# Scores of the second attention through M = Wq^T Wk, low halves of turn 1 on GpSimd, routing weights stationary

## The reference, cut to what matters

```python
x = x + _L0_xattn_ref(ctx_1024, _layernorm(x), ...)      # 8 heads of 128, keys of context and x
x = x + _L0_ffn_ref(_layernorm(x), W1, b1, W2, b2, scale)  # 256 -> 1024 -> 256, gelu, rank-one updates
x = x + _L1_xattn_ref(_layernorm(x), ctx_1024, ctx_1024, Wq_w, Wq_b, Wk_w, Wk_b, Wv_w, Wv_b)
x = x + _L1_ffn_ref(_layernorm(x), Wg, Wu, Wd, Wr, temperature)
...
Q = jnp.einsum('bsd,kd->bsk', query, Wq_w) + Wq_b        # _L1_xattn_ref: one head of 256
K = jnp.einsum('bsd,kd->bsk', key_, Wk_w) + Wk_b
V = jnp.einsum('bsd,vd->bsv', value, Wv_w) + Wv_b
attn = jax.nn.softmax(jnp.einsum('bqk,bsk->bqs', Q, K) * scale, axis=-1)
...
weights = _routing_weights(x, Wr, temperature)           # _L1_ffn_ref: x @ Wr is 256 x 8 per image
h = jax.nn.silu(x @ Wg[e]) * (x @ Wu[e])                 # 8 experts of 256, all of them, in every row
out = jnp.einsum('bte,betd->btd', weights, e_out)
```

## Time and profile before

| what | value |
|---|---|
| time, median of 3 runs (lowest to highest) | 2014.67 us (2013.67 to 2015.39) |
| the profiled execution's own time | 2019.56 us |
| its span in the trace | 2017.8 us |
| TensorE busy | 1953.7 us, 97% of the span, 14272 matmuls |
| VectorE, ScalarE, GpSimd busy | 1386.3, 1105.1, 362.4 us |
| granted clock of TensorE, mean | 0.99 |

### The profile page before, as it was taken

The page is one execution under the profiler, slowest core; times in us unless marked ns, Lnnn a source line. Parts: engine busy times, 40 slices in busy tenths (PEclk is TensorE's granted clock), DMA queues, the critical chain, the costliest instruction groups (busy, mean ns, idle before and its releaser), DMA issues.

```text
span 2017.8 us, 41686 instructions
## 1 busy us (share of the span) xinstructions
PE 1953.7 (97%) x14272; PEld 1832.0 (91%) x14272; DVE 1386.3 (69%) x3420; ACT 1105.1 (55%) x2283; POOL 362.4 (18%) x613
## 2 busy tenths in 40 slices
PE   7999999999999999999978799999999999999998
PEld 6789888888888888888878799999999999999998
DVE  7876767767777777677646656766666667666665
ACT  5655556555555556555555445544554555544553
POOL 2222222222222222222211101111111001111100
PEclk9999999999999999999989899999999999999999
DMA  4000000000000000000014000000000000000000
GB/s 160 12 22 21 10 10 21 21 21 10 10 21 21 21 10 10 21 21 10 6 38 137 11 13 17 11 17 15 13 16 16 17 11 17 11 17 11 16 7 11
DMA packets 47211, 44.51 MB, mean 22 GB/s; under 512 B 6848, under 2 KB 45376, under 8 KB 47168
## 3 DMA queue, kind: packets, MB, share of 16 engines
q1 hardware_dynamic: 47168, 43.96, 6.9%
HBM read 34.77 MB, written 8.39 MB: 21 GB/s over the span
## 4 chain that ended last, share of the span: by engine, by line
PE 86%; DVE 5%; ACT 5%; issue 2%; SPq 1%; POOL 0%; DMA 0%; ACTq 0%; DVEq 0%; POOLq 0%
PE ring L618 9%; PE ring L620 9%; PE ring L619 9%; PE ring L1749 8%; PE ring L1750 8%; PE ring L1751 8%; PE ring L671 4%; PE sim L1749 3%; PE sim L1751 3%; PE sim L1750 3%; PE sim L618 3%; PE sim L620 2%; PE sim L619 2%; PE ps_x L1749 2%; PE ps_x L1750 2%
## 5 line engine op out<-in xcount | busy, mean ns | idle before, releaser
L1749 PE MATMUL ring<-b_xch,b_weh 128*128 128x256 f32 x1024 | 294.0, 287 | 18.9 <-DVE b_wel L1376 15.8
L1750 PE MATMUL ring<-b_xcl,b_weh 128*128 128x256 f32 x1024 | 289.4, 283 | 0.0
L1751 PE MATMUL ring<-b_xch,b_wel 128*128 128x256 f32 x1024 | 289.3, 283 | 0.0
L411 ACT ACTIVATE a_pr<-sim,a_nmax 128x512 f32<-128x512 f32 x256 | 174.4, 689 | 209.4 <-DVE a_nmax L537 209.3
L326 POOL TENSOR_SCALAR a_pr<-a_pr,a_rinv 128x512 f32<-128x512 f32 x256 | 183.0, 728 | 500.3 <-DVE a_rinv L547 497.5
L1749 PEld LDWEIGHTS ring<-b_xch,b_weh 128*128 128x128 f32 x1024 | 196.9, 192 | 20.3 <-DVE b_wel L1376 16.9
L1750 PEld LDWEIGHTS ring<-b_xcl,b_weh 128*128 128x128 f32 x1024 | 197.1, 193 | 0.0
L1751 PEld LDWEIGHTS ring<-b_xch,b_wel 128*128 128x128 f32 x1024 | 196.4, 192 | 0.0
L1387 DVE TENSOR_TENSOR b_act_e<-b_act_e,ring 128x512 f32<-128x512 f32 x128 | 88.0, 688 | 134.5 <-PE ring L1751 121.1
L1117 ACT ACTIVATE b_act_e<-ring 128x512 f32<-128x512 f32 x128 | 76.6, 599 | 169.1 <-PE ring L1751 168.7
L528 DVE TENSOR_TENSOR a_ptl<-ring,a_pth 128x512 fp32r<-128x512 f32 x256 | 163.6, 680 | 3.1 <-ACT a_pth L401 2.0
(11 more groups left out here) (355 smaller groups left out, 6285.9 us busy)
## 6 DMA issues: line engine op xcount, KB each, us to landing
a_c_in<-in_ctx_in SPq DMA_DIRECT2D x16, 256.0 KB, 2.7
a_x_in<-in_x SPq DMA_DIRECT2D x16, 256.0 KB, 2.9
a_x_res<-in_x SPq DMA_DIRECT2D x16, 256.0 KB, 2.7
x_between<-a_x_out SPq DMA_DIRECT2D x16, 256.0 KB, 2.2
b_x_s<-x_between SPq DMA_DIRECT2D x16, 256.0 KB, 2.6
b_up<-b_ev SPq DMA_DIRECT2D x256, 1.0 KB
out_x<-b_acc SPq DMA_DIRECT2D x16, 256.0 KB, 2.2
b_ct_raw<-in_ctxT SPq DMA_DIRECT2D x15, 256.0 KB, 2.6
```

Of the source, the lines that this page charges most:

```text
L411: nc.scalar.activation(pr[:, h % 2, t, :], sim[t][:], ACT.Exp, bias=nmax[:, h % 2, t:t + 1], accum_out=rsum[:, h % 2, t:t + 1]).then_inc(e ...
L1749: nc.tensor.matmul(out, lh, rh, start=(n == 0), stop=False)
L1750: nc.tensor.matmul(out, lh, rl, start=False, stop=False)
L1751: last = nc.tensor.matmul(out, ll, rh, start=False, stop=(n == len(parts) - 1 and not more))
```

## The change

- **M.** With Q = x Wq^T + bq and K = c Wk^T + bk the scores are (x M + u) c^T, u = Wk^T bq, plus a number for each row of the query, x v + s. M = Wq^T Wk, u, v and s are formed once (`fold`, 18 matmuls for v and the sums and 12 for M, where image 0's keys were), and M takes Wq's place in the queries' product (`q_fill`). The keys' product and its halves are gone; the scores' moving operand is cth, ctl. The row number cancels in the softmax; the kernel forms it on GpSimd (`row_shifts`) and ScalarE (`row_shift_sums`) and VectorE adds it to the maximum and takes it off again (`maxima`).
- **Turn 1.** `expert_low` of experts 2 to 7 moves from VectorE to GpSimd's queue, experts 2 to 5 ahead of rstd B, 6 ahead of rstd A, 7 ahead of the odd rows. Their high halves move one slot ahead (`WARM_AT`), the first ahead of silu 1.
- **Routing.** Wr, its halves in 16 of 128 columns and zeros behind, is the stationary operand: 4 matmuls with 256 columns ahead of expert 0's gate, a copy by ScalarE (`r_copy`) and 2 transposes (`r_turned`) behind its up.
- **Order.** `v_fill` moves from behind `y_update` to behind gate 4, and its halves to the slot of silu 4. In the passage image 0's fourth gelu moves from ahead of head 2's probabilities to behind K4, and the context's split from head 2 to head 4.

```diff
...
-    Q, K, V, PT = (slice(n, n + 3, 2) for n in (0, 1, 4, 5))
...
+    Q, V, PT = (slice(n, n + 3, 2) for n in (1, 4, 5))
+    mh, (wk_raw, ml) = put("w_queries", "mh", [P, DC, D], F32R, odd=1), put("w_queries", "ml", [P, DC, D], F32R, raw=True,
+                                                                        odd=1)
...
+    cth, (wq_raw, ctl) = put("w_queries", "cth", [P, DC, S], F32R, odd=0), put(
+        "w_queries", "ctl", [P, DC, S], F32R, raw=True, odd=0)
+    once = {"K": (wk_raw, mh, ml), "Q": (wq_raw, cth, ctl), "V": (wv_raw, wvh, wvl)}
+    v_b, rt = put("w_queries", "v_b", [P, D]), put("w_queries", "rt", [P, S])
+    wr = put("w_queries", "wr", [P, DC, P], F32R)
+    bk_wide = xth[:].rearrange("p c (z m) -> p c z m", z=2)
...
-    WARM_AT = {2: 0, 3: 1, 4: 2, 5: 3, 6: 4, 7: 5}
+    WARM_AT = {2: 0, 3: 1, 4: 2, 5: 2, 6: 3, 7: 4}
...
+        def row_shifts(n):
+
+            pool.wait_ge(ln_ready["B"], n + 1)
+            nc.gpsimd.tensor_tensor(pr[:], ln[:], v_b[:].unsqueeze(1).to_broadcast([P, ST, D]), ALU.mult)\
+                .then_inc(shift_in, 1)
...
+            if (h, done) == (3, "probs"):
+                pool.wait_ge(first.sems["ring_full"], first.fill_count(2, ("Q", 3)))
+                nc.gpsimd.memset(f32(wr[:]), 0.0).then_inc(consts, 1)
+                pool.wait_ge(w_ready, 6)
+                pool.wait_ge(consts, 3)
+                nc.gpsimd.tensor_copy(wr[:, :, 0:2 * E].rearrange("p c (z e) -> p c z e", z=2), f32(wr_two[:]))\
+                    .then_inc(consts, 1)
+                pool.wait_ge(full["H", 3], 1)
+                nc.gpsimd.tensor_copy(bk_wide, f32(bqk[:, 1]).unsqueeze(3).to_broadcast([P, DC, 2, P]))\
+                    .then_inc(consts, 1)
             if (h, done) == (4, "probs"):
+                pool.wait_ge(uv_step, 2)
+                row_shifts(0)
                 bias_x2(0)
...
             def turn(t, chain, more, warm):
+                if warm:
+                    for e in (2, 3, 4, 5):
+                        expert_low(e)
                 if chain:
                     rstd_of(t, "B")
+                    row_shifts(t)
                     bias_x2(t)
+                if warm:
+                    expert_low(6)
                 if more:
                     rstd_of(t + 1, "A")
                     bias_x1(t + 1)
+                if warm:
+                    expert_low(7)
+                if more:
                     odd_rows(t + 1)
...
+        def folded_high():
+            act.wait_ge(m_full, 2)
+            nc.scalar.activation(mh[:], halves(OWN["M"]), ACT.Copy, scale=QSCALE).then_inc(wqkv_hi, 1)
+
+        def row_shift_sums(t):
+            act.wait_ge(shift_in, t + 1)
+            for k in range(ST):
+                last = nc.scalar.activation(pr[:, k, :], pr[:, k, :], ACT.Identity, bias=shift[:, 0:1],
+                                            accum_out=row_shift[:, k:k + 1])
+            last.then_inc(shift_ready, 1)
...
+
+        def r_copy(t):
+            act.wait_ge(full["R"], 2 * t + 1)
+            nc.scalar.activation(rt[:], ring[BANK["R"]][:, 0:S], ACT.Copy).then_inc(hi["R"], 1)
...
-            if (h, done) == (2, "begin"):
+            if (h, done) == (2, ("K", 4)):
                 gelu_high(0, 3)
-            if (h, done) == (2, ("T", 2, 1)):
-                context_high(0)
...
             if (h, done) == (4, ("K", 6)):
-                biased_high(0, "K", K, bk_s)
+                folded_high()
+                context_high(0)
...
             if (h, done) == (5, "exps"):
-                biased_high(0, "Q", Q, bq_s)
+                act.wait_ge(uv_step, 2)
+                row_shift_sums(0)
+                queries_high(0)
...
+                r_copy(0)
...
+                for e in warm_in(0) if warm else ():
+                    for j in range(3):
+                        expert_high(e, j)
                 silu(i, 1)
                 routing_exps(i)
                 hidden_high(i, 1)
                 if chain:
-                    for n in range(HC // 2):
-                        gelu_high(t, n)
-                for e in warm_in(0) if warm else ():
-                    for j in range(3):
-                        expert_high(e, j)
-
-                silu(i, 2)
-                if chain:
-                    context_high(t)
-                hidden_high(i, 2)
+                    gelu_high(t, 0)
+                    gelu_high(t, 1)
                 for e in warm_in(1) if warm else ():
                     for j in range(3):
                         expert_high(e, j)
                 if chain:
+                    gelu_high(t, 2)
+                    gelu_high(t, 3)
...
+                for e in warm_in(2) if warm else ():
+                    for j in range(3):
+                        expert_high(e, j)
...
-                if chain:
-                    biased_high(t, "K", K, bk_s)
-                    copy_high(t, "V", hh[:, V, 0:S])
...
                 for e in warm_in(3) if warm else ():
                     for j in range(3):
                         expert_high(e, j)
...
+                if chain:
+                    copy_high(t, "B", xth[:])
+                    copy_high(t, "V", hh[:, V, 0:S])
+                hidden_high(i, 4)
+                for e in warm_in(4) if warm else ():
+                    for j in range(3):
+                        expert_high(e, j)
+                if chain:
+                    queries_high(t)
+                    row_shift_sums(t)
...
+        def folded_biases():
+
+            dve.wait_ge(m_full, 1)
+            nc.vector.tensor_scalar(v_b[:], OWN["UV"][:, 0:D], QSCALE, None, ALU.mult)
+            nc.vector.tensor_reduce(sums[:], OWN["UV"][:, D:D + 6].rearrange("p (n z) -> p n z", z=2), AX.X, ALU.add)\
+                .then_inc(uv_step, 1)
+            dve.wait_ge(uv_step, 1)
+            nc.vector.tensor_scalar(shift[:], sums[:, 0:1], QSCALE / D, None, ALU.mult)
+            nc.vector.tensor_scalar(sums[:, 1:3], sums[:, 1:3], QSCALE, None, ALU.mult).then_inc(uv_step, 1)
+
+        def folded_low():
+            dve.wait_ge(wqkv_hi, 4)
+            nc.vector.scalar_tensor_tensor(ml[:], halves(OWN["M"]), QSCALE, f32(mh[:]), ALU.mult, ALU.subtract)\
+                .then_inc(wqkv_lo, 1)
...
+            dve.wait_ge(max_ready, 2 * t + 1)
+            dve.wait_ge(shift_ready, t + 1)
+            for k in range(ST):
+                last = nc.vector.scalar_tensor_tensor(peak[:, k:k + 1], nmax[:, k:k + 1], row_shift[:, k:k + 1],
+                                                      row_shift[:, k:k + 1], ALU.subtract, ALU.add)
+            last.then_inc(max_ready, 1)
...
             if (h, done) == (4, ("K", 6)):
                 norm_apply(0, "B", x2_s)
-                biased_low(0, "K", K, bk_s)
+                folded_biases()
+                folded_low()
+                context_low(0)
...
             if (h, done) == (4, ("T", 4, 1)):
+                dve.wait_ge(shift_in, 1)
                 norm_apply(1, "A", x1_s)
...
-                for e in warm_in(0) if warm else ():
-                    for j in range(3):
-                        expert_low(e, j)
...
                 if chain:
-                    biased_low(t, "K", K, bk_s)
                     norm_apply(t, "B", x2_s)
-                    copy_low(t, "V", hl[:, V, 0:S], hh[:, V, 0:S])
...
                 if chain:
                     copy_low(t, "B", xtl[:], xth[:])
+                    copy_low(t, "V", hl[:, V, 0:S], hh[:, V, 0:S])
                 hidden(i, 4)
                 if more:
+                    dve.wait_ge(shift_in, t + 1)
                     norm_apply(t + 1, "A", x1_s)
                 hidden_low(i, 4)
-                for e in warm_in(3) if warm else ():
...
                 if chain:
-                    biased_low(t, "Q", Q, bq_s)
+                    queries_low(t)
...
+        def fold():
+
+            v, sums_at = OWN["UV"][:, 0:D], OWN["UV"][:, D:D + 6]
+            product(v, range(DC), lambda c: bk_wide[:, c, 0, :], lambda c: bk_wide[:, c, 1, :], lambda c: cth[:, c, :],
+                    lambda c: ctl[:, c, :])
+            for n in range(3):
+                for c in range(DC):
+                    for z, w in enumerate((mh, ml)):
+                        st = bk_wide[:, c, z, :] if n == 0 else w[:, c, (n - 1) * P:n * P]
+                        last = nc.tensor.matmul(sums_at[:, 2 * n:2 * n + 2], st, bqk[:, 0, c, :],
+                                                start=(c == 0 and z == 0), stop=(c == DC - 1 and z == 1))
+            last.then_inc(m_full, 1)
+            cd = halves(OWN["M"])
             for k in range(DC):
                 cols = slice(k * P, (k + 1) * P)
-                last = product(cd[:, k, :], range(DC), lambda c: wqkvh[:, w, c, cols], lambda c: wqkvl[:, w, c, cols],
-                               lambda c: rh[:, c, :], lambda c: rl[:, c, :])
-            last.then_inc(full[name], 1)
```

(43 more changed lines are left out.)

162 lines of the change are left out of this document (69 added, 93 removed).

## The result

The changed kernel takes 1989.37 us (median of 4 runs, 1987.67 to 1991.09); the kernel before, timed beside it, 2015.03 (2013.67 to 2017.28). The ratio is 0.987, 95% interval 0.986 to 0.9884: 25.7 us less, where 30 were forecast (1984.7, range 1966 to 2003). The profiled executions stand 28.5 us apart in their spans (2017.8 and 1989.3), since the one of before lay 4.5 us above its median and the one of after 1.7.

A forecast was written before the change was run, and what follows sets the result against it. TensorE, busy 97% of a 2017.8 us span, was taken as the bound; gains of 13.0 (loop turns 2 to 15), 16 (turn 1) and 1 (passage) make 30 us off the 2014.67 median: 1984.7 us, range 1966 to 2003.

The forecast's parts named there:

- The bound: Whole kernel: TensorE, busy 97% of 2017.8 us, sets the time; busy time removed counts in full wherever it doesn't wait.
- Loop: routing 0.13 us: Loop turns 2 to 15: the new routing product with 2 transposes saves TensorE 0.13 us per turn.
- Loop: a new wait at transposes B of 0.60 us: Loop turns: TensorE arrives earlier at transposes B and waits 0.60 us for VectorE's normalisations, leaving 0.93 us gain per turn.
- Costs put at nothing: Loop: row shifts on GpSimd, row sums on ScalarE and the maximum correction lie in idle time and cost nothing.
- Turn 1: 68 us: Second loop's turn 1: falls from 84.3 to 68 us, a gain of 16, with two long waits of 2.5 and 4.5.
- The clock term: Turn 1: each us of long wait costs 0.75 us more through the lower clock; 7.0 us of waits cost 5.2.
- 24 (no long wait): Turn 1: the upper end of its forecast gain, 24 us, if no long wait comes.
- Passage: a gain of 1: Passage between the halves: M's longer chain against the moved fourth gelu, net gain 1 us, ends 4 lost and 4 gained.
- (2): Loop and turn 1: neither the wait at B nor the one at the scores comes; gain 46, 1968 us, chance 0.20.
- (3): GpSimd's SBUF lock stalls VectorE: turn 1 gives 8 and the loop 5 us; 2001 us, chance 0.20.
- (4): Loop: keys' matmuls were hidden, a VectorE and ScalarE chain sets the turn; only turn 1 gains; 1998 us, chance 0.05.
- (5): Turn 1: GpSimd's rounding subtraction costs far more than its addition; slower overall from 3.8 us each; chance 0.05.

## Why the prediction was right, point by point

- **The bound.** Right. TensorE's matmuls count in full (twelve put back: +1.41 less the wait they fill). My window for a turn ended 0.26 us short of the next routing product (56.66 instead of 56.92 us); in the differences this cancels, but "55.7 us per turn" should have read 56.0, against 56.12 measured.
- **Loop: keys 1.40 us.** Right; their place in the earlier trace rows was 1.41 us wide.
- **Loop: routing 0.13 us.** Measured 0.09 by the experiment that undoes it.
- **Loop: a new wait at transposes B of 0.60 us.** Right in place and cause, a little small. The profile puts 0.54 us there, and that itself understates it:

```profile
1418.50 0.28 PE L1820 MATMUL ps_c<-b_wvh,b_ctl 128*128 128x256 f32 x1
...
1418.84 0.28 PE L1820 MATMUL ps_c<-b_wvh,b_ctl 128*128 128x256 f32 x1
1419.65 0.63 PE L1829 MATMUL sim<-ident,b_ln 128*128 128x128 f32 x4 [0.54 <-DVE b_ln L1420]
...
1418.77 0.73 DVE L1420 TENSOR_SCALAR b_ln<-b_x_s,b_mv,b_rows 128x256 f32<-128x256 f32 x2 [0.86 <-POOL b_rows L1033]
```

  The last matmul of the values' product starts at 1418.84 and the next could have started 0.117 later, at 1418.96; the transposes start at 1419.65, 0.69 late. The idle time is counted from the end of the last matmul, which lasts 0.28 us, over twice its distance to the next. Taking the wait away gave 0.71 us in one experiment, and 0.73 in the other. What the forecast had too small is the signal: the normalisations end at 1419.50 and the transposes start 0.15 us later, where 0.05 stood. So a turn gained 0.80 us where 0.93 stood, and 14 turns 10.8 for 13.0. Most of these 2.2 us are the wait; 0.4 come from turns 11 to 14 of the kernel before, which were 0.1 us shorter than the turn that I had measured. With the 0.6 lost ahead of the passage, and 1.2 of turn 1 and 0.1 of the tail on the other side, it makes the 1.5 us between 30 and the profile's 28.5; the other 2.8 lie between the profiled executions and the medians.
- **Costs put at nothing** (row shifts, row sums, maximum correction in the loop). Right: without them no turn of the loop is shorter.
- **Turn 1: 68 us.** 67.28 by the window. The two long waits are those named: 3.2 us for the gelu's low half (2.5 forecast), 3.1 for the queries' (4.5 forecast); no wait for the experts' low halves; GpSimd's 1.31 us for 1.5. Undoing the part cost 16.9 us where 16 were forecast. The sum is better than its terms. The gelu wait had a second cause that I had left to a rival: 1.5 us of it is VectorE's routing weights standing behind GpSimd. Another 0.7 goes away with the old routing product. The queries' wait was 1.4 us too large by three small things. The "lock or two" (0.4) didn't come. GpSimd's queue from B to the end of rstd A took 7.7 us and not 8.0, with expert 6 as forecast (4.2 for 4.3). And TensorE came to the scores 7.5 us after B and not 7.0:

```profile
1134.01 1.29 POOL L1050 TENSOR_TENSOR b_pr<-b_ln,b_v_b 128x512 f32<-128x512 f32 x1 [0.85 <-DVE b_ln L1420]
...
1136.52 4.18 POOL L1072 TENSOR_TENSOR b_wel<-b_wel_raw,b_weh 128x512 fp32r<-128x512 f32 x3
...
1141.06 0.71 POOL L1033 TENSOR_TENSOR b_rows<-b_rows,mhalf 128x2 f32<-128x2 f32 x1
```

  The clock term, 0.75 us for each us waited, is the weak one. It was a mean over the five waits of before, each with its fall, and there is no such proportion: two falls cost 4.0 us, where 5.2 stood, and the table has the same waits with more, less or nothing. That the term came near is luck. The rest of the turn is 56.9 us (67.28 less 6.4 and 4.0) where 55.7 stood, which hides it. And the best case of the forecast's range, "24 (no long wait)", doesn't follow from its own terms: a turn of 55 to 56 us is 28 to 29 less than 84.3, and 24 is the case with the gelu wait left.
- **Passage: a gain of 1.** 0.98 us measured, by cancellation of larger terms than I had: undoing the gelu's move cost 5.4 us (2.0 of waiting, and 3.4 with two falls of the clock), and M's longer chain cost 4.4 (85.96 with the gelu in its old place, 81.56 before, both with the two falls), where I had 3. Of the gelu's 3.4 us of clock only the first fall is surely its own, as shown above; with that one alone it gave 3.8. That the forecast of 1 came out is luck. The 4.4 include the context's split, moved from head 2 to head 4; no run separates it from M's chain. Nor was the values' product, which the change also moved, put back by itself.
- **Rivals.** (2), no new waits, fell by the trace; but an order of the same work nearly without them exists, and its 1971 us is near the 1968 that stood there. (3), the lock, is real in turn 1, where it cost 1.5 us of waiting and, with the clock, 5.5. In the loop of the changed kernel it costs nothing that a run shows, but only by the order: the residual bias behind rstd A brought it there too. By the rule that the Trainium skill gives (SBUF — State Buffer, "SBUF: two separate sides"), an operation of VectorE that needs the shared ports waits for GpSimd's whole instruction if that one started first. The 1.78 us for 0.68 above agree. That its price stayed low because VectorE had idle time around most such meetings is my reading; VectorE was busy 40.85 of turn 1's 67.28 us. (4) fell with the twelve matmuls, (5) with 1.31 us.

## What to carry to other kernels

When work is removed from the engine that sets the time, ask how far ahead of the next wait it stood: here 12 matmuls of 1.41 us were worth 0.7 less, until 6 others took their place. Price an order by each queue's own line (what stands ahead of rstd A on GpSimd, what ahead of the gelu on ScalarE); those sums held to 0.7 and 1.4 us. And undo a part that "gains 1" before calling it small: here it was 5.4 against 4.4, with 3.4 of the 5.4 in falls of the clock. Keep falls of the clock apart from waits in such a sum: two kernels with equal waits can differ by one.
